# A two-layer attention and feed-forward kernel: rows normalised on GpSimd in the first eight pairs, two PSUM copies moved to ScalarE, and TensorE's transposes put earlier

## What is computed

```
x = L0_attn_x                                  # (8, 512, 256) fp32
xn = layernorm(x)
x = x + attention(xn) + int8_linear(xn)        # layer 0
xn = layernorm(x)
x = x + gated_compare(xn) + rwkv_ffn(xn)       # layer 1
```

## Time and profile before

| | us |
|---|---|
| median of 3 runs | 1048.55 (1047.62 to 1048.55) |
| the profiled execution's own time | 1048.61 |
| its span in the profile | 1046.8 |
| busy: PE | 997.9 (95%) |
| busy: DVE | 846.8 (81%) |
| busy: POOL | 766.6 (73%) |
| busy: ACT | 758.2 (72%) |

### The profile page before, as it was taken

How to read it: one execution, slowest core, us unless ns; L and a number is a source line. 1 busy time by engine, 2 the same in 40 slices (tenths; PEclk the granted TensorE clock), 3 DMA queues, 4 the chain that set the end, 5 groups by cost and what they waited for, 6 DMA issues and landing times.

```text
span 1046.8 us, 23671 instructions
## 1 busy us (share of the span) xinstructions
PE 997.9 (95%) x7974; PEld 673.3 (64%) x7974; DVE 846.8 (81%) x2272; ACT 758.2 (72%) x2014; POOL 766.6 (73%) x941
## 2 busy tenths in 40 slices
PE   5878998999999999999999999999999998999998
PEld 4545555666666666666666666666666765777776
DVE  7979889877878888877787777877787766998875
ACT  5968887666666767766666676666666766999994
POOL 3766667868787877787787878777867645878884
PEclk9989999999999999999999999999999999999999
DMA  8723444343333343234333333433333100000101
GB/s 273 231 82 112 142 132 134 92 132 92 111 108 92 97 117 99 90 114 119 92 92 111 92 97 91 122 97 91 99 101 96 52 1 1 22 22 21 34 30 41
DMA packets 99703, 98.70 MB, mean 94 GB/s; under 512 B 13312, under 2 KB 95360, under 8 KB 98944
## 3 DMA queue, kind: packets, MB, share of 16 engines
q1 hardware_dynamic: 99584, 97.19, 30.4%
HBM read 56.25 MB, written 40.90 MB: 93 GB/s over the span
## 4 chain that ended last, share of the span: by engine, by line
PE 71%; DVE 15%; ACT 7%; issue 4%; POOL 2%; DMA 1%; ACTq 0%; DVEq 0%; SPq 0%; POOLq 0%
PE bank L1640 22%; PE bank L1723 13%; PE bank L1737 12%; PE bank L1754 7%; PE bank L1711 6%; PE bank L1712 5%; PE bank L1929 2%; ACT arena L869 2%; PE bank L1875 1%; DVE arena L1516 1%; POOL arena L628 1%; DVE arena L1362 1%; DVE arena L1378 1%; DVE arena L1340 1%; DVE arena L1342 1%
## 5 line engine op out<-in xcount | busy, mean ns | idle before, releaser
L628 POOL TENSOR_SCALAR arena<-arena,rc 128x128 f32<-128x128 f32 (+3 forms) x512 | 275.4, 556 | 198.2 <-DVE rc L1371 198.2
L869 ACT ACTIVATE arena<-arena,nm 128x256 f32<-128x256 f32 (+3 forms) x512 | 283.4, 554 | 74.5 <-DVE nm L1362 69.1
L1362 DVE CUSTOM_DVE_ANT_0 arena<-bank,mask_rows 128x256 f32<-128x256 f32 (+3 forms) x512 | 232.9, 482 | 79.0 <-PE bank L1712 78.4
L1723 PE MATMUL bank<-ident,arena 128*128 128x128 f32 x1280 | 222.7, 280 | 20.1 <-DVE arena L1378 14.4
L1723 PEld LDWEIGHTS bank<-ident,arena 128*128 128x128 f32 x1280 | 149.1, 140 | 87.6 <-DVE arena L1378 52.1
L877 ACT ACTIVATE arena<-bank 128x512 f32<-128x512 f32 (+3 forms) x256 | 108.5, 424 | 65.6 <-PE bank L1723 65.5
L1737 PE MATMUL bank<-arena 128*64 128x512 f32 (+3 forms) x1024 | 153.1, 441 | 0.0
L1712 PE MATMUL bank<-arena 128*128 128x256 f16 (+3 forms) x512 | 152.9, 299 | 0.0
L1711 PE MATMUL bank<-arena 128*128 128x256 f16 (+3 forms) x512 | 139.9, 300 | 1.9 <-DMA arena<-scr 1.9
L1378 DVE COPY arena<-bank 128x512 f32<-128x512 f32 (+3 forms) x256 | 124.8, 487 | 20.6 <-PE bank L1723 16.8
L1737 PEld LDWEIGHTS bank<-arena 128*64 128x64 f32 x1024 | 68.1, 137 | 96.0 <-issue 71.6
(11 more groups left out here) (173 smaller groups left out, 2201.6 us busy)
## 6 DMA issues: line engine op xcount, KB each, us to landing
arena<-scr SPq DMA_DIRECT2D x320, 128.0 KB, 2.7
scr<-arena SPq DMA_DIRECT2D x256, 128.0 KB, 1.7
arena<-in_weights SPq DMA_DIRECT2D x5, 1024.0 KB, 7.5
x_sb<-in_x SPq DMA_DIRECT2D x8, 512.0 KB, 8.6
out<-x_sb SPq DMA_DIRECT2D x16, 256.0 KB, 2.2
xscr<-arena SPq DMA_DIRECT2D x12, 256.0 KB, 3.0
xsh<-xscr SPq DMA_DIRECT2D x6, 256.0 KB, 3.6
xsl<-xscr SPq DMA_DIRECT2D x6, 256.0 KB, 4.1
```

Of the source, the lines that this page charges most:

```text
L628: last = pool.tensor_scalar(pr[slot][:, OFF[i]:OFF[i + 1]], pr[slot][:, OFF[i]:OFF[i + 1]], rc[:, slot, i:i + 1], 1.0, ALU.mult, ALU.mult)
L869: act.activation(pr[slot][:, OFF[i]:OFF[i + 1]], pr[slot][:, OFF[i]:OFF[i + 1]], ACT.Exp, scale=-1.0, bias=nm[:, slot, i:i + 1], accum_out ...
L1362: dve.tensor_tensor_reduce(pr[slot][:, OFF[i]:OFF[i + 1]], s_tile[i], mask_rows[:, SQ - P * (i + 1):SQ], -1.0, -MASKED, ALU.add, ALU.min, ...
L1723: last = pe.transpose(banks[5 + h][:, (i - j) * P:(i - j + 1) * P], pr[2 * par + h][:, OFF[i] + j * P:OFF[i] + (j + 1) * P], ident[:])
```

## The change

- GpSimd normalises the rows of batch n+1 in ring n (0 to 6), between `low_o` and `normalise(n + 1, 0)`. ScalarE keeps only batch 0's.
- In rings 1 to 7 ScalarE copies the transposes j = 0 and j = 2 of head 1, which VectorE copied before.
- In all rings TensorE issues `pt(n, 0, 1)` ahead of the Wo products and `columns_of_rows(n, 0)`, and both `pt(n, 2, h)` ahead of the second group of them.
- The roots of batches 1 to 7 are cut in pieces: the guess at the end of ring -1 (before `inverse(0, 1)`), two Newton steps in `first_gap(0)`, the last step in `second_gap(0)`. Their running value lies in PSUM (bank 1) and not in SBUF.
- `row_maximum(0)` goes to the end of ring 0, `row_maximum(1)` to `first_gap(1)`; one `part_maximum` per ring in rings 1 to 4; Wo's scale, `low_part` and `quantise` go from the gaps to the ends of rings 5 to 10.
- The clearing of `kz[1]` goes behind GpSimd's four table products. The last `fill` of 50 becomes 40 pairs of 64-column products with alternating weights. The last `av3` finishes one bank after the other, and `final` starts on the first.

```diff
@@ gpsimd
             last.then_inc(diag_done, 1)
-            pool.memset(kz[1], 0.0).then_inc(kz_zero, 1)
...
                 last.then_inc(tab_done, 1)
+            pool.memset(kz[1], 0.0).then_inc(kz_zero, 1)
...
+            def normal_rows(b):
+                pool.wait_ge(roots_done, 2)
+                after(pool, amax_done, b - 1)
+                after(pool, xt1_done, KT * (b - 1))
+                pool.sem_inc(pool_passed, 1)
+                for c in range(NT):
+                    t = b * NT + c
+                    pool.tensor_scalar(xn1[b % 2][:, c, :], x_sb[:, t, :], nw3[:, 0, t:t + 1], nbx[:, t:t + 1],
+                                       ALU.mult, ALU.add).then_inc(xn1_done, 1)
@@ gpsimd ring
                 low_o(n + AHEAD - 1)
+                if 0 <= n < NB - 1:
+                    normal_rows(n + 1)
@@ scalar ring
                 exps(n + 1, 0, e, (0, 2))
                 if 1 <= n < NB:
+                    pt_whole(n, 0, 1)
                     columns_high(n, 0)
...
-                if 1 <= n < NB - 1:
-                    normal_rows(n + 1, (0,))
                 pt_whole(n, 2)
+                if 1 <= n < NB:
+                    pt_whole(n, 2, 1)
...
-                if 0 <= n < NB - 1:
-                    normal_rows(n + 1, (2, 3) if n else range(NT))
@@ vector: roots
-                dve.tensor_tensor(t2, y0, y0, ALU.mult).then_inc(s, 1)
+                dve.tensor_tensor(t2, y0, t1, ALU.mult).then_inc(s, 1)
...
-                dve.scalar_tensor_tensor(out=t2, in0=t2, scalar=-0.5, in1=t1, op0=ALU.mult, op1=ALU.mult).then_inc(s, 1)
+                dve.scalar_tensor_tensor(out=t2, in0=t2, scalar=-0.5, in1=y0, op0=ALU.mult, op1=ALU.mult).then_inc(s, 1)
@@ vector: first_gap
-                if 0 <= n < NB and n != 1:
+                if n == 0:
+                    roots(later_tiles, 1, (1, 2), wo)
+                elif n < NB and n > 0:
                     row_maximum(n)
...
-                elif n == 8:
-                    low_part(0)
-                elif n == 9:
-                    quantise(0, 1)
-                elif n == 10:
-                    low_part(2)
@@ vector: second_gap
-                    dve.wait_ge(act_stats, NB - 3)
-                    inverse_roots(slice(1, NB), 1)
+                    roots(later_tiles, 1, (3,), wo)
+                    roots_bias(later_tiles)
...
-                elif 1 <= n <= 3:
-                    if n == 1:
-                        row_maximum(1)
+                elif 1 <= n <= 4:
                     part_maximum(n - 1)
-                    if n == 3:
-                        part_maximum(3)
@@ vector: ring_end
-                if n == 7:
+                if n == 0:
+                    row_maximum(0)
+                elif n == 5:
+                    column_maximum(slice(G_O, G_L), 2)
+                    weight_scale(slice(G_O, G_L), 2)
+                elif n == 7:
                     quantise(0, 0)
+                    low_part(0)
                 elif n == 8:
                     input_scale()
+                    low_part(1)
                 elif n == 9:
-                    quantise(0, 3)
+                    for step in range(1, 4):
+                        quantise(0, step)
+                elif n == 10:
+                    low_part(2)
+                    low_part(3)
@@ vector: pt_whole, ring
-                if absent(n):
+                if absent(n) or 1 <= n < NB and j % 2 == 0:
                     return
...
+                if n == -1:
+                    dve.wait_ge(act_stats, NB - 3)
+                    roots(later_tiles, 1, (0,), wo)
                 inverse(n + 1, 1, e)
@@ tensor ring
                 scores(n + 1, 0, (0, 2))
+                pt(n, 0, 1, o)
...
-                pt(n, 0, 1, o)
                 scores(n + 1, 0, (3,))
...
                 scores(n + 1, 1, (1,))
+                pt(n, 2, 0, o)
+                pt(n, 2, 1, o)
...
-                pt(n, 2, 0, o)
-                pt(n, 2, 1, o)
                 scores(n + 1, 1, (0, 2))
@@ tensor: body3
-                av3(n, 3, u)
+                if n == NB - 1:
+                    av3_by_bank(n, 3, u)
+                else:
+                    av3(n, 3, u)
```

More of the change, by code:

```diff
@@ L745, in columns_high, with first_rows @@
                 act.activation(columns(b)[0][:, k], src[:], ACT.Copy).then_inc(xth_done, 1)
[L747 to L754, removed]
+            def first_rows():
+                act.wait_ge(roots_done, 1)
+                for t in range(NT):
+                    act.activation(xn1[0][:, t, :], x_sb[:, t, :], ACT.Identity, bias=nbx[:, t:t + 1],
                                    scale=nw3[:, 0, t:t + 1]).then_inc(xn1_done, 1)
@@ L786, in weights_high @@
                 act.activation(wgroup(wh, g), staged(g), ACT.Copy, scale=inv[:, g:g + 1]).then_inc(done, 1)
-            normal_rows(0, range(NT))
+            first_rows()
             act.wait_ge(rows_mm, 1)
@@ L1105, in statistics, with roots @@
                 dve.wait_ge(st3_step, base + STAT_STEPS)
-            def roots(tiles, turn, parts=range(NEWTON + 1)):
+            def roots(tiles, turn, parts=range(NEWTON + 1), bank=None):
                 y0, t1, t2 = nw3[:, 0, tiles], nw3[:, 1, tiles], nw3[:, 2, tiles]
+                out = y0
+                if bank is not None:
+                    y0 = bank[:, tiles]
                 for part in parts:
@@ L1113, in roots @@
                     else:
-                        root_step(d1, turn * ROOT_STEPS, part - 1, y0, t1, t2)
+                        root_step(d1, turn * ROOT_STEPS, part - 1, y0, t1, t2, out if part == NEWTON else y0)
             def normal_rows(b, out, done, count):
@@ L1138, in inverse_roots @@
                 roots_bias(tiles)
+            later_tiles = slice(NT, NB * NT)
             def row_maximum(b):
@@ L1271, in second_gap @@
                 elif n == 0:
[L1272 to L1273 removed]
+                    roots(later_tiles, 1, (3,), wo)
+                    roots_bias(later_tiles)
                     dve.tensor_scalar(bvs[:], vec[:, V_BV:V_BV + NP], inv[:, G_V:G_V + 1], None, ALU.mult)
[L1275 to L1277 removed]
+                elif 1 <= n <= 4:
                     part_maximum(n - 1)
[L1279 to L1290 removed]
+                elif n == 6:
+                    dve.tensor_tensor(sc_vo[:], sc[:, G_V:G_V + 1], sc[:, G_O:G_O + 1], ALU.mult)
                 elif 13 <= n < 17:
@@ L1532, in final @@
                     return
-                after(dve, av3_mm, made(4, n, 3))
+                after(dve, av3_mm, made(4, n, 3 + w if n == NB - 1 else 3))
                 after(dve, yx_done, made(2, n, w))
@@ L1623, in fill, with fill_short @@
                     pe.matmul(pt1[:, 0:P], identb[:], maskb, start=True, stop=True)
+            def fill_short(count):
+                for _ in range(count):
+                    for a, z in ((identb, maskb), (maskb, identb)):
+                        pe.matmul(pt1[:, 0:L], a[:], z[:, 0:L], start=True, stop=True)
             pe.wait_ge(diag_done, 1)
@@ L1769, in ffn @@
                             f_mm if t == 1 else None)
-            FILL = (0, 60, 0, 50)
+            FILL = (0, 60, 0, 40)
             def ring(n):
@@ L1795, in ring @@
                 if -AHEAD < n < -1:
-                    fill(FILL[n + AHEAD])
+                    (fill_short if n == -2 else fill)(FILL[n + AHEAD])
                 evens(n + AHEAD)
@@ L1926, in av3, with av3_terms @@
                     after(pe, o3_done, made(2, n - 1, 1))
+                av3_terms(j, par, range(NT)).then_inc(av3_mm, 1)
+            def av3_terms(j, par, tiles):
                 for a, (pp, vv) in enumerate(((pt3h, xn3h[par]), (pt3h, xn3l[par]), (pt3l, xn3h[par]))):
-                    for t in range(NT):
+                    for t in tiles:
                         last = pe.matmul(banks[4 + t // 2][:, t % 2 * D:(t % 2 + 1) * D], pp[:, j, t * P:(t + 1) * P], vv[:, j],
@@ L1931, in av3, with av3_by_bank @@
                                          stop=(j == NT - 1 and a == 2 and t % 2 == 1), skip_group_check=True)
-                last.then_inc(av3_mm, 1)
+                return last
+            def av3_by_bank(n, j, par):
+                after(pe, pt3l_done, made(4, n, j))
+                for w in range(2):
+                    av3_terms(j, par, (2 * w, 2 * w + 1)).then_inc(av3_mm, 1)
             def body3(n, u):
```

6 lines of the change are left out of this document (2 added, 4 removed).

## The result

The changed kernel takes 1035.95 us (median of 4 runs, 1035.79 to 1036.21), the kernel before 1048.1 beside it (4 runs): ratio 0.9884, 95% interval 0.9867 to 0.9902. The profiled execution spans 1034.1 us, before 1046.8. One execution of one variant (experiment 2) took 2593.26 us, for a reason that no trace shows; every other one of all runs lies between 1026 and 1060.

The account below looks back on a forecast made before the run. Early rings were taken as bound by a VectorE, GpSimd, ScalarE chain, rings from 10 on by TensorE's own work. Terms -0.8 - 3.8 - 1.3 - 0.3 - 0.6 = -6.8 took 1048.6 to 1041.8 us, range 1037.5 to 1046.

Parts of the forecast that it names:

- All later rings: 0: Rings from 11 on: the moved transposes find their operands ready, so no new wait and no gain, 0 us.
- rival 2: Rings from 11 on: a moved transpose finds its operand late and every ring pays; at 0.3 us each 1057.8; chance 0.08.
- Start: 0.8: Setup: moving GpSimd's clearing frees VectorE's first root instruction; about 0.8 us gets through, limited by the second load.
- Ring 0: 3.8: Ring 0: even_terms starts 2.45 us earlier and six products run at full clock, 1.3 less; together 3.8 us gained.
- Rings 1 to 7: 1.3: Rings 1 to 7: side jobs leave the chain, ScalarE's new copy adds 3.4, the clock gives 1.2; net 1.3 us gained.
- Rival 1: Rings 1 to 7: ScalarE's new copy is not on the chain, 3.4 us more gained, 1038.4; chance 0.17.
- GpSimd's rows: Rings with moved normalisation: four tiles at 0.5 us each, hidden in GpSimd's idle time if below 0.85 a tile.
- rival 3: GpSimd's rows take longer than 0.85 us a tile; at 1.16 each, 8.7 us lost, 1050.5; chance 0.06.
- The term of ring 6: Ring 6: ScalarE's last rows leave the chain, 0.98 us gained.
- Rings 8 to 10: 0.3: Side jobs leave the gaps: 1.0 us gained in rings 8 and 9, 0.7 lost in ring 10; net 0.3 gained.
- rival 4: TensorE's clock falls again after waits: one fall costs 2.5 us, 1044.3; two give 1046.8; chance 0.09.
- End: 0.6: Kernel's end: half of the last twelve products finish earlier, hiding two of final's four tiles; 0.6 us gained.

Follow-up runs that it names:

- experiment 2: Kernel before with only pt(n, 2, 0) and pt(n, 2, 1) moved to their new place from ring 8 on: 1050.15 us, ratio 1.0015.
- experiment 5: Kernel before, old order, VectorE's j = 0 copy of head 1 cut to 256 of 512 columns from ring 8 on: 1035.83 us, ratio 0.9884.
- experiment 1: Kernel before with only pt(n, 0, 1) moved to its new place from ring 8 on: 1038.77 us, ratio 0.9909.
- experiment 4: Changed kernel with all three moved transposes back at their old places from ring 8 on: 1044.07 us, ratio 0.9957.
- experiment 13: Kernel before, old order, VectorE's j = 0 copy of head 1 cut to 384 of 512 columns from ring 8 on: 1041.63 us, ratio 0.9936.
- experiment 8: Changed kernel with the three moved transposes at their old places from ring 59 on: 1033.93 us, ratio 0.9865.
- experiment 9: Changed kernel with the later rows' inverse roots in one piece again, in ring 0's second gap: 1039.83 us, ratio 0.9921.
- experiment 6: Changed kernel with head 1's j = 0 copy kept on VectorE in rings 1 to 7: 1033.21 us, ratio 0.9856.
- experiment 7: Changed kernel with ScalarE's j = 0 copy of head 1 placed ahead of high_e in rings 1 to 7: 1034.05 us, ratio 0.9863.
- experiment 10: Changed kernel with the later batches' rows normalised by ScalarE again, at their old places: 1038.32 us, ratio 0.9909.
- experiment 12: Changed kernel, j = 0 copy on VectorE, old transpose order from ring 59, four part_maximum at the ends of rings 1 to 4: 1034.04 us, ratio 0.9871.

## Why the prediction was wrong, step by step

- **All later rings: 0.** This is the step that failed: "From 206 to 860 us TensorE is busy 649.65 of 654.00 us: the rings from 10 on are TensorE's own work, and nothing that frees another engine helps there", and from it "So no new wait, no gain: 0." A VectorE copy 0.27 us shorter gained 10.5 us there (experiment 5). The busy time of the matmuls covered a wait of 0.26 us in each ring; the move of `pt(n, 0, 1)` took it away: 0.24 us in most rings, less or nothing in eight of rings 20 to 29, 9.3 us in 47 (experiments 1, 4, 5, 13). The same view had 433.38 us of weight loads for 649.65 of matmuls, and the weight loads' waits name VectorE's copy. I asked of each moved transpose only whether its own operand was ready, and not what stands behind it for the bank that it fills. The Trainium skill (Perfetto Trace Analysis, "Identifying the Most-Contended Engine") warns of that first reading: the busy share of matmuls is no good measure of how near TensorE is to its limit; the share of its peak rate that the products reach and the busy share of weight loads are. The trace agrees in the direction: 99% of that window was matmuls and 66% weight loads, and 1.6% of the late rings' time could go. How much can go neither share tells; the waits of the weight loads do.
- **No new wait in the later rings** held for rings 11 to 57, but for rings 25 to 29, whose gain is between 0.07 and -0.23 us. It didn't hold for the last rings, which I didn't look at. Rings 60 to 62 lost 1.9 us and the last six 2.0, 1.7 of it by `pt(n, 2, *)` (experiments 2 and 8). This is rival 2 in three rings of 53.
- **Start: 0.8**, measured 0.65 (from one execution of each; the setup varies by more than this from kernel to kernel, so the size isn't shown). The row that takes the second half of the maxima begins at 12.06, 0.03 behind the end of the load, as argued.
- **Ring 0: 3.8**, measured 3.97. `bvs` ends at 62.74 where the forecast had 63.4; the clock stayed up. Undoing this edit brings a clock of 0.82 back (experiment 9). Start and ring 0 together, 4.62 here, hold over all traces: the first `av` has its median at 70.9 us in the six kernels with the old start and at 66.4 in the nine with the new start and ring 0, 4.5 earlier, where 4.6 were forecast.
- **Rings 1 to 7: 1.3**, measured 0.26. Rings 2 to 4 (13.66, as 12.58 + 0.49 + 0.6) were right. Ring 1 gained 2.45 (15.09 to 12.64) where 1.83 were forecast (1.12 + 1.2 - 0.49), but the old ring 1 takes 13.92 to 15.36 us in six traces, so 0.6 is within what varies. Rings 5 to 7 should have been 13.07 each and are 13.65, 13.49 and 13.66, 1.6 more together. Two things were left out. `sc_vo`, a tensor_tensor that went from ring 5's gap to ring 6's, takes 0.58 on the chain though it is one column wide: it ends with GpSimd's `low_o` beside it (143.53 + 0.58 = 144.11; 142.94 + 1.16 = 144.10). In the kernel before, where GpSimd was idle, it took 0.16. And in rings 5 and 7, without a side job on VectorE, another path is longer: ScalarE's copy, TensorE's three transposes, the six products of `evens`, then the even terms (the chain of waits, rings 5 and 6):

```profile
127.89 0.49 ACT arena L887
128.42 0.55 PE bank L1739 x3
128.97 1.31 PE bank L1656 x6
130.30 0.75 DVE arena L1347
...
143.53 0.58 DVE sc_vo L1286
```

  I had forecast TensorE's wait ahead of `pt(n, 1, 1)` (1.7 us; measured 10.0 in seven places, 1.4 in the mean and 1.6 at most) but not followed the products behind it. Rival 1 is refuted (experiments 6 and 7).
- **Rings 8 to 10: 0.3**, measured 0.43, as 0.13, 0.63 and -0.33. The signs are the forecast ones (1.0 gained in rings 8 and 9, 0.7 lost in ring 10), the sizes smaller.
- **GpSimd's rows: hidden, 0.5 us a tile.** The row has 552 ns, below the 0.85 us of rival 3, and no ring's chain goes through it; rival 3 is refuted. The term of ring 6 was too small in the new surroundings (experiment 10).
- **The clock** stayed at 1.00 behind ring 0; rival 4 didn't come.
- **End: 0.6.** The last `final` comes 12.90 us earlier than in the earlier trace rows, the one of the batch before it 12.24, so the 0.66 is there; but between the first and the second batch of layer 1 0.35 is lost, and `final` itself is 0.18 longer (timeline of VectorE). From the last `av` of layer 0 to the end, nine of the ten kernels with this layer 1 take 187.61 to 188.02 us and the tenth (experiment 7, with a granted clock of 0.66 from 865 to 870 us) 189.10, the kernel before 188.08; so the 0.35 is within what varies, and why it varies stays open:

```profile
1029.64 1.84 DVE L1548 SCALAR_TENSOR_TENSOR x_sb<-bank,arena,x_sb 128x256 f32<-128x256 f32 x4 [1.28 <-PE bank L1949]
```

The sum of forecast terms before the late rings, 6.2 with the start, is near the measured 5.3, partly by luck: ring 1 gave 0.6 more than its terms and rings 5 to 7 gave 1.6 less. The miss is the one line with a zero.

## What to carry to other kernels

When matmuls look saturated, read the waits of the weight loads, and the row of a merged group of transposes against the time to the next instruction: here a wait of 0.26 us was invisible in the busy time, and it added up over 47 rings. For every instruction that is moved, ask three things: is its operand there, what does its result release for the next user of the same bank, and whose queue (SyncE's too) stands in order behind it. And price the new wait together with the work that stands behind it on the engine that waits.

## What was not expected of the hardware

- A tensor_tensor on one column (`sc_vo`) took 0.58 us on the chain, and `bvs`, 8 columns, 1.18; both end within 0.02 us of GpSimd's `low_o` beside them. For `bvs` this was forecast, for `sc_vo` it wasn't. In the kernel before, with GpSimd idle, they took 0.16 and 0.22, and the Newton steps of the changed kernel, 4 and 28 columns, took 0.16 to 0.19.
- A stretch with a wait of 3.8 us on TensorE had its clock at 0.82 (experiment 9), and waits of 1.4 us in the mean in seven successive rings left it at 1.00. With a wait of 5.1 us in experiment 12 it was 0.51 for some 7 us.
- An unchanged setup differs from kernel to kernel: the first `av` began at 66.40 in the changed kernel, and at 65.68 to 67.93 in its variants with the same setup and ring 0. Ring 1 of the kernel before and of its variants with the same ring 1 varied by 1.4 us; where it was short, the granted clock from 66 to 74 us was 0.79 and not 0.57.
